# The normalisation of each attention task's output on GpSimd instead of VectorE, in a decoder layer

## The reference

```python
x = _layernorm(x + self_attention(x))            # 16 heads of 8 features, biases on q, k, v and output
x = _layernorm(x + cross_attention(ctx, x, ctx)) # one 8x8 matrix per q, k, v shared by all heads
x = _layernorm(x + ffn(x))                       # two int8-quantised linear layers, 128 -> 512 -> 128, with gelu
def _layernorm(x, eps=1e-05):                    # no weights
    m = mean(x); v = var(x)
    return (x - m) / sqrt(v + eps)
```

## Time and profile before

| | |
|---|---|
| Median of 3 runs | 393.32 us (392.85 to 394.03) |
| The profiled execution | 393.29 us |
| Its span | 391.6 us (1.7 us lie around it) |
| Mean granted TensorE clock | 0.894 of full speed |
| Busy: DVE | 333.2 us, 85% of the span, 730 instructions |
| Busy: PE, PEld | 269.2 us (69%), 173.4 us (44%) |
| Busy: ACT | 255.1 us (65%) |
| Busy: POOL | 176.5 us (45%), 331 instructions |
| Attention in full swing | about 80 to 280 us |
| Last attention slots and extremes | about 280 to 302 us |
| Feed-forward part | about 302 us to the end |

### The profile page before, as it was taken

How to read it: one execution, slowest core, us unless ns; L and a number is a source line. 1 busy time by engine, 2 the same in 40 slices (tenths; PEclk the granted TensorE clock), 3 DMA queues, 4 the chain that set the end, 5 groups by cost and what they waited for, 6 DMA issues and landing times.

```text
span 391.6 us, 13163 instructions
## 1 busy us (share of the span) xinstructions
PE 269.2 (69%) x4889; PEld 173.4 (44%) x4890; DVE 333.2 (85%) x730; ACT 255.1 (65%) x507; POOL 176.5 (45%) x331
## 2 busy tenths in 40 slices
PE   4565636988888898898998898888871265103850
PEld 3343424556556565565665565555541222001530
DVE  4665428999999999999999999999987389998984
ACT  2124434787787887887887887777761398606675
POOL 1676053665566566666656656666122081000000
PEclk9999856999999999999999999999995576855995
DMA  1440022332332323323324223332000000000024
GB/s 47 109 128 22 28 66 60 84 91 71 104 86 83 99 83 88 105 76 100 96 66 118 85 78 104 99 93 64 16 5 0 0 1 0 0 0 3 0 83 133
DMA packets 48998, 25.19 MB, mean 64 GB/s; under 512 B 6440, under 2 KB 48808, under 8 KB 48936
## 3 DMA queue, kind: packets, MB, share of 16 engines
q1 hardware_dynamic: 48216, 24.02, 21.6%
q10 hardware_dynamic: 720, 0.33, 0.3%
HBM read 9.39 MB, written 2.10 MB: 29 GB/s over the span
## 4 chain that ended last, share of the span: by engine, by line
DVE 30%; issue 26%; PE 19%; POOL 9%; ACT 8%; DMA 3%; SPq 3%; ACTq 1%; POOLq 0%; DVEq 0%
DVE neg_max L749 15%; PE ps L984 5%; PE ps L1010 4%; PE ps L1044 4%; DVE arena_q L871 3%; ACT probs L582 2%; DMA arena_h<-parts_sk 2%; SPq L339 2%; ACT y_out L650 2%; POOL arena_h L452 2%; POOL rstd L463 2%; DVE r_sum L759 2%; PE ps L1052 2%; ACT arena_h L622 1%; PE ps L1032 1%
## 5 line engine op out<-in xcount | busy, mean ns | idle before, releaser
L749 DVE TENSOR_REDUCE neg_max<-ps 128x8 f32<-128x1024 f32 x128 | 157.4, 1230 | 26.0 <-PE ps L984 24.1
L984 PE MATMUL ps<-arena_h 31*128 31x128 f16 x1024 | 53.8, 225 | 44.9 <-DVE neg_max L749 24.8
L582 ACT ACTIVATE probs<-ps 128x1024 f32<-128x1024 f32 x64 | 65.6, 1025 | 23.1 <-PE ps L991 21.6
L540 ACT ACTIVATE probs<-ps 128x1024 f32<-128x1024 f32 x64 | 65.5, 1024 | 19.5 <-PE ps L991 17.9
L984 PEld LDWEIGHTS ps<-arena_h 31*128 31x128 f16 x1024 | 31.5, 96 | 78.3 <-DVE neg_max L749 40.8
L991 PE MATMUL ps<-arena_h 32*128 32x128 f16 x1024 | 52.7, 222 | 0.5 <-ACT probs L540 0.5
L460 POOL TENSOR_TENSOR var_eps<-mean_var,eps_col 128x1 f32<-128x1 f32 x64 | 12.1, 190 | 88.9 <-DVE mean_var L790 88.9
L1010 PE MATMUL ps<-probs,arena_q 128*32 128x128 f32 x1024 | 44.3, 294 | 0.0
L1010 PE MATMUL ps<-probs,arena_h 128*32 128x128 f32 x1024 | 41.2, 279 | 0.2 <-ACT probs L540 0.2
L463 POOL TENSOR_TENSOR rstd<-var_eps,minus_half 128x1 f32<-128x1 f32 x64 | 35.5, 555 | 5.0
L991 PEld LDWEIGHTS ps<-arena_h 32*128 32x128 f16 x1024 | 30.1, 95 | 1.6 <-issue 0.9
(11 more groups left out here) (142 smaller groups left out, 627.8 us busy)
## 6 DMA issues: line engine op xcount, KB each, us to landing
arena_h<-parts_sq SPq DMA_DIRECT2D x48, 64.0 KB, 1.9
arena_h<-parts_ck SPq DMA_DIRECT2D x48, 64.0 KB, 2.0
arena_h<-parts_cq SPq DMA_DIRECT2D x48, 64.0 KB, 1.9
arena_h<-parts_sk SPq DMA_DIRECT2D x45, 64.0 KB, 1.9
xT_in<-in_xT_dram SPq DMA_DIRECT2D x16, 128.0 KB, 2.5
xN_in<-in_xN_dram SPq DMA_DIRECT2D x16, 128.0 KB, 2.3
cT_in<-in_cT_dram SPq DMA_DIRECT2D x16, 128.0 KB, 2.7
cN_in<-in_cN_dram SPq DMA_DIRECT2D x16, 128.0 KB, 2.4
```

The lines of the kernel that those rows point to most:

```text
L540: act.activation(probs[1][:, :], ps_s2, ACT.Exp, scale=SCALE).then_inc(ex, 1)
L582: act.activation(probs[0][:, :], ps_s2, ACT.Exp, scale=SCALE).then_inc(ex, 1)
L749: dve.tensor_reduce(neg_max[b.par][:, HH * half:HH * half + HH], ps_s1.rearrange("p (h k) -> p h k", h=HH), AXX, ALU.max, negate=True).the ...
L984: ins = pe.matmul(ps_s1[:, at:at + S], q[r:r + MAX_AT, j, :], kk[r:r + MAX_AT, j, :], start=True, stop=True, skip_group_check=True)
```

## The change

The `tensor_scalar` of L766 is taken out of DVE's slot and put into POOL's slot, behind the power of L463, with a wait on POOL's own `rq`. POOL's wait for `xn` at L462 goes. DVE gets a wait for `xn` ahead of the residual sum, so that `y_sb` isn't overwritten before POOL has read it. The operation, its operands, their shapes and the semaphore that it raises are the same.

```diff
@@ POOL, slot(k), v = task(k - 4)
                     pool.wait_ge(ve, v.pos + 1)
-                    need(pool, xn, v.pos - 1)
                     pool.tensor_tensor(rstd[v.par][:, :], var_eps[v.par][:, :], minus_half[:, :], ALU.pow).then_inc(rq, 1)
+                    pool.wait_ge(rq, v.pos + 1)
+                    if v.kind == "S":
+                        dst, src = in_groups(x1_all[:, v.m, :]), by_group(y_sb[v.par][:, :])
+                    else:
+                        dst, src = x2_all[:, v.m, :], y_sb[v.par][:, :]
+                    pool.tensor_scalar(dst, src, mean_var[v.par][:, 0:1], rstd[v.par][:, :],
+                                       ALU.subtract, ALU.mult).then_inc(xn, 1)
@@ DVE, slot(k), between the reciprocal (L759) and the product (L771)
-                if v is not None:
-                    dve.wait_ge(rq, v.pos + 1)
-                    if v.kind == "S":
-                        dst, src = in_groups(x1_all[:, v.m, :]), by_group(y_sb[v.par][:, :])
-                    else:
-                        dst, src = x2_all[:, v.m, :], y_sb[v.par][:, :]
-                    dve.tensor_scalar(dst, src, mean_var[v.par][:, 0:1], rstd[v.par][:, :],
-                                      ALU.subtract, ALU.mult).then_inc(xn, 1)
@@ DVE, slot(k), x = task(k - 3), ahead of the residual sum (L786)
+                    need(dve, xn, x.pos - 1)
                     dve.tensor_tensor(dst, own, residual, ALU.add).then_inc(yy, 1)
```

More of the change, by code:

```diff
@@ L740, in slot @@
             def slot(k):
-                b, w, x, v = task(k + 2), task(k - 2), task(k - 3), task(k - 4)
+                b, w, x = task(k + 2), task(k - 2), task(k - 3)
                 def maximum(half):
```

## The result

| | before | after |
|---|---|---|
| Median of the runs beside each other | 393.09 us (4 runs, 392.81 to 394.03) | 402.90 us (4 runs, 399.98 to 404.26) |
| The profiled execution, its span | 393.29 us, 391.6 us | 402.33 us, 400.6 us |
| Busy: DVE | 333.2 us, 730 instructions | 323.6 us, 666 instructions |
| Busy: POOL | 176.5 us, 331 instructions | 227.8 us, 395 instructions |
| Busy: PE | 269.2 us | 276.4 us |

The changed kernel is slower by 2.35% (ratio 1.0235, 95% interval 1.0175 to 1.0296); the forecast was 390.7 us. The loss lies in the attention part. The last row maximum starts at 281.62 us before and at 289.95 after, 8.3 us later; the other 0.7 us of the 9.0 between the spans come behind it.

The account below looks back on a forecast made before the run. It took the attention part to be bound by a ring in which PE and DVE wait for each other. From 393.29 us, less 3.3 (first gaps) and 0.3 (tail), plus 1.0 (cq delay), it forecast 390.7; range 389.3 to 393.6.

Parts of the forecast that it names:

- The gain: Attention slots: without the normalisation on DVE, 17 first gaps between its reductions shrink to 0.50 us, together 3.3 us.
- the twelve gaps of 0.67: First gaps in slots where POOL adds the residual bias while DVE normalises: to become 0.50 us, gaining 12 x 0.17 = 2.04.
- the one of 0.87: First gap at 88 us, with the longest normalisation, 0.667 us: to become 0.50, gaining 0.87 - 0.50 = 0.37.
- the four late ones: First gaps of 0.71 us in four late slots, from 244 us: to shrink, gaining 4 x 0.21 = 0.84 us.
- I take the gain as kept: Second half of those slots: PE's 0.25 us wait moves with the reduction if ACT and stacks are earlier still.
- I take 0.35, between the first two: Length in us of POOL's normalisation, between rows of 0.282 and 0.398; everything behind it on POOL comes 0.47 us later.
- The biases, ck, sq and sk have more than 0.5 us to spare: POOL's work behind the normalisation: these have that room or stand behind a wait on ACT; only split cq has not.
- The cost of a delay: Late cq stacks: 1.0 us at a delay of 0.47, 0.8 at 0.40, some 3 at 0.85.
- The third: Rival: cq stack becomes the bound at over about 1.1 us of delay, POOL late too; 396.3 us, chance 0.12.
- The second: Rival: POOL's operation is slow, some 0.7 us, and the cq delay costs 3 us; 392.7 us, chance 0.12.
- The fourth: Rival: code fetched for POOL's new operation, first normalisation some 7 us late; 392.7 us if once, chance 0.04.
- The drop of DVE's busy time: Sign to look for: it falls by some 23 us, mostly turning into waits for PE at L749.

Follow-up runs that it names:

- e4: The changed kernel with twelve extra operations on POOL in one slot, to time POOL's forms; 408.42 us in its one run, of use for its rows alone.
- e3: The changed kernel, but POOL normalises only 4 of the 128 columns; 395.13 us, ratio 1.0052 to the kernel before.
- e7: The changed kernel with only 17 normalisations on POOL, where DVE had set the first gap, and 47 on DVE; 395.96 us, ratio 1.0053 to the kernel before.
- e9: As e7, with POOL's residual bias put after the split ck instead of before it; 392.99 us, ratio 0.9966 to the kernel before.
- e13: The changed kernel with 127 already served waits more on PE ahead of the attention; 399.28 us, ratio 1.0126 to the kernel before.
- e1: The kernel before, with POOL also normalising into a spare tile while DVE keeps its own normalisation; 401.62 us, ratio 1.0179.

## Why the prediction was wrong, point by point

**The gain: right in place, not kept.** DVE's first gap is 0.51 where it was 0.67, as forecast. Ten of the twelve gaps of 0.67 and the one of 0.87 are at 0.50 to 0.51 in the trace of after, the four late ones at 0.50 to 0.58; two of the twelve are longer, 0.77 and 1.02. In the changed kernel the gain is spent in the second gaps. "I take the gain as kept" rested on ACT and the stacks being earlier by more than the gain, and for the stacks that wasn't looked up.

**The operation: mis-sized.** "I take 0.35, between the first two": it is 0.80, above even my upper bound of 0.73. The rows that I took as near were near in shape alone. L424 is another operation, and the `tensor_tensor` rows have neither column operands nor two ALU steps; `e4` shows that both are paid. That a power of one column takes 0.55 and an add of one column 0.19 was the warning that the kind of operation counts on POOL, and not its elements alone. The page that I had set against the move also came out too kind: the Trainium skill (GPSIMD Engine Reference, section 4.1, Engine selection) puts one input near VectorE's rate; measured are 0.80 us against 0.25.

**"The biases, ck, sq and sk have more than 0.5 us to spare": the step that failed most.** sk made 8.1 of the 12.6 us. Already at the delay of 0.5 in `e3`, the size that I had forecast, PE waits 4.2 us for sk where it had waited 1.3. The row was there: PE's scores at 162.88 in the earlier trace rows name parts_sk as the last to come. I read it as the reduction's round trip. Of the eleven S pairs from the sixth on, four had their keys landed no more than 0.15 us ahead of the reduction's end, or after it, already before. And ck has no room either, since SP has its DMAs ahead of cq's (`e7`, `e9`).

**The cost of a delay: linear, from margins taken one by one.** I had 1.0 us at a delay of 0.47, some 3 at 0.85. At 0.93 it was 10.3 more of waiting, by both stacks, and 7.4 on DVE's timeline. `e3`, with a delay of 0.5, has 7.3 us of stack waits, 5.0 more than before. The term is too small by a factor of two and a half to five. One of the two stacks was left out, and a stack that lands late by itself makes a delay count in full; how the factor divides between the two isn't shown. The clock's 3.2 us stood in no term.

**The rivals.** The third had the mechanism and the sign (a stack as the bound, deciding from a delay of 0.9 us); at 396.3 us it had a loss of 3.0 us where 9.6 came (its price for the stacks, 6.6, against 7.4 and the clock's 3.2), and it left the sk stack out too. The second named the slow operation, and gave it 392.7. "Decides from 0.9" was also too late: `e3` is already slower than before. The fourth is excluded: POOL was idle for 0.11 us at most ahead of any of the 64 new instructions, the first included.

**What held:** POOL never gets late for good (it still waits 26.4 us for the mean and variance), PE names the stack DMAs more often, DVE's freed time shows in its gaps. The drop of DVE's busy time, 9.6 us and not 23, was mis-sized: the normalisation overlaps the reciprocal by 0.09 and the product by 0.07 us in the earlier trace rows, and taken off 0.36, 64 times, that leaves 12.8. Most of the remaining 3.2 comes back where the product had overlapped the next reduction by 0.08 us (161.22 + 0.28 against 161.42) and now ends before it.

## What to carry to other kernels

Before work is moved to an engine with much idle time, follow each thing behind it on that engine to the instruction that waits for it, and take the one with the least room, through the DMA queue's order as well; a busy share says nothing of this. An instruction that is longer in some slots than in others may be slowed by what runs beside it on a neighbour engine: here moving that neighbour's instruction and two loads gave 1% together, and moving the slow one in 17 tasks as well gave nothing that could be measured; moving it in all 64 tasks of the kernel before cost 2.4%. Price an operation by a row of its own kind, with the same operands; where there is none, take a range up to several times the nearest, and ask what happens at its far end first.

## What the runs showed of the hardware that I had not expected

**Instruction fetches delay DMAs.** Queue q8 brings 16 KB of instructions, 41 times in the kernel before, about each 6 us in full swing. A 64 KB copy into a stack lands after 1.9 to 2.3 us without one beside it and after up to 4.0 with one. The Trainium skill (Runtime: NRT & Kernel Launch, section Instruction fetch mechanics) has a sequencer refill its instructions in blocks of 16 KB, 256 instructions, through a DMA queue of its own, at a cost that is mostly hidden. The trace agrees: PE's queue has 10,444 of the kernel's 13,163 instructions (matmuls, weight loads and 665 others), which is 40.8 times 256 for 41 packets, and from one packet to the next PE starts 255 instructions on average. `e13` moves the late landings with PE's count. So a fetch costs the DMAs beside it time; whether it costs PE any isn't told by these rows.

**DVE beside POOL.** A `tensor_scalar` of 128x128 on DVE takes 0.25 us alone. In the kernel before it takes 0.47 beside POOL's bias and 0.50 beside the values of a C pair, without either waiting for a semaphore. Timelines of DVE and POOL:

```profile
168.22 0.50 DVE L766 TENSOR_SCALAR x_all<-y_sb,mean_var,rstd 128x128 f32<-128x128 f32 x1
```

```profile
167.88 0.75 POOL L492 TENSOR_TENSOR arena_h<-cN_in,zero_col 128x128 f32<-128x128 f32 x2
```

DVE's instruction ends at 168.72, 0.09 us after POOL's at 168.63; beside the bias it ends 0.08 after it too (161.29 against 161.21). This holds for all 12 biases, and beside a split as well, which is mostly over so soon that 0.25 to 0.30 us are enough. Where a split had just begun, near 88 us, the normalisation took the 0.667 of the earlier trace rows. So this DVE instruction waits POOL's out. The reciprocal (0.25), which reads PSUM, shows no such stretch beside the same instructions. The Trainium skill (Trainium Architecture — The Big Picture, section What this means for kernel authors) has the two share a port pair under an exclusive lock; the trace agrees.

**A wait of PE can cost a clock level.** After PE waits of 1.6, 1.9 and 2.1 us (ending at 87, 150 and 268 us of after) the granted clock went from 1.00 to 0.50 for 3.4 us. A wait of 1.5 us at 229 us was not followed by a fall, nor one of 1.8 us at 188 us in `e1`; so the length of one wait doesn't decide it alone.
